# The preparation of a cross-attention and feed-forward kernel, rebuilt: paired 64-row matmuls for K, V and VW, w1 by halves, some parts of the second batch put off, other DMA queues

## The chip, the cores and the metric

The kernel runs on 1 core of a Trainium2 chip. The metric is device time in microseconds (us); lower is better. Before the change the median of 3 runs is 190.82 us (190.44 to 191.01).

## The reference

```python
x = x + xattn(layernorm(x), ctx)      # x (2, 1024, 256), ctx (2, 77, 192)
#   q = x @ Wq (256, 512); k, v = ctx @ Wk, ctx @ Wv (192, 512); 8 heads of 64
#   softmax(q k^T / 8) v, then @ Wo (512, 256) + bo
x = x + ffn(layernorm(x))
#   h = layernorm(x) * gamma + beta
#   y = silu(h @ dequant(fc1_q) + fc1_bias)         # 256 -> 1024
#   x + 0.5 * (y @ dequant(fc2_q) + fc2_bias)       # 1024 -> 256
#   dequant(q, s) = (q - 128) * s, one row of scales for each 128 rows
```

The second layernorm of x stands in front of the ffn, which has one of its own. All is fp32.

## The kernel before

Every engine has its own instruction list written out by hand, and semaphores tie the lists together. A matmul on large operands is made of three with fp32r operands: every operand is split into a rounded part (`_hi`) and what is left (`_lo`), and hi*hi, hi*lo and lo*hi are accumulated. ScalarE (ACT) mostly makes the `_hi` part out of PSUM, and VectorE (DVE) or GpSimd (POOL) subtracts it to give `_lo`.

The 2048 rows of x are eight pieces `a` = 0 to 7 of 256 rows (two tiles j = 0, 1 of 128); pieces 0 to 3 are batch 0, pieces 4 to 7 batch 1. For each piece, TensorE (PE) does XT (transpose x), S (`scores`, 24 matmuls), PT (transpose the probabilities), AO (`attention_out`, 30), HT (transpose the normalised rows hn), F1 (`fc1`, 48) and F2 (`fc2`, 48). The loop runs these in a software pipeline: `fc2` of piece a-1 stands ahead of `scores` of piece a+1.

**Preparation.** Since the context has only 77 rows, the weights are folded once: ctx is transposed (ctxT), K = ctx Wk and V = ctx Wv are made (`project`), Wq is transposed and centred (`transpose_wq`, `sum_wq`, `center_wq`), and then M = Wq K^T (`make_m(b, c)`, batch b, half c of the 256 inputs) and VW = V Wo (`make_vw(b, n)`) for each batch. `scores` then needs only x and M, and `attention_out` only the probabilities and VW. The row bo of the bias is put into VW by two DMAs. The ffn weights w1 and w2 are dequantized (L315 on POOL, L621 on DVE) and split (L439, L489 on ACT; L320 on POOL, L627 on DVE).

Matmuls of the preparation are plain fp32: the trace has two records for each. `make_m` already uses 64 of the 128 rows of the array for each matmul (one head each), in pairs whose two members write different PSUM banks.

PSUM has six named places (S0, S1 of two banks, H0, H1, T0, T1). A table `order` lists who fills each place in turn; `emptied(name)` on PE waits until the previous user was freed by DVE. `fc2(0, 0)` uses T0, which `AO1.0` used before it, and this is freed by `add_attention(1, 0)` (L590) on DVE. In its loop `fc2` waits for `y_lo_done`, the four parts of y_lo that POOL makes (`lower_y`, L310), at its 1st, 7th, 13th and 19th matmul.

Names in the rows: `w_hi`, `w_lo` are w1 or w2, `q_sb` their integers (later the dequantized values), `hT_lo` the lower part of the transposed hn (`split_h`, L607 and L609), `probs` the scores.

## Time and profile before

| | us |
|---|---|
| median of 3 runs | 190.82 |
| profiled execution | 190.24 |
| its span in the trace | 188.5 |
| what lies around the span | 1.74 |

The page counts how long each engine was busy: PE 182.1 us (97%), DVE 123.5 (66%), ACT 122.6 (65%), POOL 115.6 (61%). A busy share over the whole span says nothing about a stage; the views used below are those of stretches, of waits and of single instructions in order of time.

### The profile page before, as it was taken

What the parts mean: (1) busy time and instruction counts of PE and PEld (TensorE: products, weight loads), DVE (VectorE), ACT (ScalarE), POOL (GpSimd) and SP (SyncE); (2) the same over time, 40 slices, a digit from 0 to 9 for tenths busy, and PEclk for the clock granted to TensorE, in tenths of its full rate; (3) what the DMA queues carried; (4) which work ended last, traced back from release to release, by engine and by line L of the source; (5) the groups of instructions that cost most, each with busy time, mean ns of one, the idle gap of its engine ahead of it and who ended that gap; (6) DMA issues with size and microseconds to landing.
All of it is one profiled execution on the core that took longest, in us unless ns stands there. A gap on an engine that the chain in (4) does not pass through costs nothing.

```text
span 188.5 us, 3884 instructions
## 1 busy us (share of the span) xinstructions
PE 182.1 (97%) x1502; PEld 178.2 (95%) x1502; DVE 123.5 (66%) x261; ACT 122.6 (65%) x230; POOL 115.6 (61%) x159
## 2 busy tenths in 40 slices
PE   7999899799899999999999999999999999999994
PEld 7999699699899999999999999999999999998994
DVE  0287988999879374946496459746693768165341
ACT  3287970699728980898288935895389718952580
POOL 5032998479984976298709971697359753767020
PEclk9999999999999999999999999999999999999999
DMA  6996990000000100010001000100000000100101
GB/s 166 331 403 171 354 349 14 2 0 3 2 0 0 59 0 0 3 56 0 3 0 56 3 0 0 47 16 0 3 27 29 0 3 0 56 3 0 56 3 56
DMA packets 9480, 10.72 MB, mean 57 GB/s; under 512 B 2268, under 2 KB 8183, under 8 KB 9335
## 3 DMA queue, kind: packets, MB, share of 16 engines
q1 hardware_dynamic: 8837, 9.70, 15.4%
q10 hardware_dynamic: 626, 0.79, 1.4%
q8 instruction: 12, 0.20, 0.5%
q14 instruction: 5, 0.04, 0.1%
HBM read 8.38 MB, written 2.10 MB: 56 GB/s over the span
## 4 chain that ended last, share of the span: by engine, by line
PE 70%; DVE 10%; POOL 8%; DMA 7%; SPq 2%; issue 1%; ACT 0%
PE H L831 21%; PE T L843 21%; PE S L798 11%; PE T L819 11%; DMA s_sb<-in_L_ffn_fc_scales 7%; PE S L805 3%; PE S L751 3%; POOL w_lo L320 3%; POOL q_sb L315 3%; DVE w_lo L627 2%; DVE hT_lo L609 2%; POOL probs L278 1%; DVE q_sb L621 1%; POOL rstd L289 1%; DVE probs L567 1%
## 5 line engine op out<-in xcount | busy, mean ns | idle before, releaser
L310 POOL TENSOR_TENSOR y_lo<-y,y_hi 128x512 fp32r<-128x512 f32 x28 | 37.6, 1364 | 2.9 <-ACT y_hi L430 2.8
L278 POOL TENSOR_TENSOR probs<-probs,rsum 128x616 f32<-128x616 f32 x16 | 19.1, 1217 | 32.1 <-DVE rsum L579 32.0
L831 PE MATMUL H<-hT_hi,w_hi 128*128 128x256 f32 x128 | 37.3, 291 | 1.3 <-issue 0.8
L843 PE MATMUL T<-w_hi,y_hi 128*128 128x256 f32 x128 | 36.6, 286 | 0.6 <-DVE w_lo L627 0.6
L831 PE MATMUL H<-hT_lo,w_hi 128*128 128x256 f32 x128 | 35.5, 277 | 0.0
L843 PE MATMUL T<-w_lo,y_hi 128*128 128x256 f32 x128 | 35.5, 277 | 0.0
L831 PE MATMUL H<-hT_hi,w_lo 128*128 128x256 f32 x128 | 35.4, 277 | 0.0
L843 PE MATMUL T<-w_hi,y_lo 128*128 128x256 f32 x128 | 35.4, 277 | 0.0
L426 ACT ACTIVATE y<-H,vec 128x256 f32<-128x256 f32 x64 | 26.5, 467 | 8.1 <-PE H L831 8.1
L399 ACT ACTIVATE probs<-probs,rstd 128x616 f32<-128x616 f32 x16 | 12.9, 807 | 27.2 <-DVE probs L567 27.2
L831 PEld LDWEIGHTS H<-hT_hi,w_hi 128*128 128x128 f32 x128 | 24.1, 188 | 2.1 <-issue 1.2
L584 DVE TENSOR_TENSOR pT_lo<-S,pT_hi 128x640 fp32r<-128x640 f32 x16 | 13.1, 822 | 18.9 <-ACT pT_hi L403 18.9
L843 PEld LDWEIGHTS T<-w_hi,y_hi 128*128 128x128 f32 x128 | 24.1, 188 | 0.8 <-DVE w_lo L627 0.8
L843 PEld LDWEIGHTS T<-w_lo,y_hi 128*128 128x128 f32 x128 | 24.1, 188 | 0.0
L831 PEld LDWEIGHTS H<-hT_lo,w_hi 128*128 128x128 f32 x128 | 24.1, 188 | 0.0
L843 PEld LDWEIGHTS T<-w_hi,y_lo 128*128 128x128 f32 x128 | 24.0, 188 | 0.0
L831 PEld LDWEIGHTS H<-hT_hi,w_lo 128*128 128x128 f32 x128 | 24.0, 188 | 0.0
L819 PE MATMUL T<-vw_hi,pT_hi 128*128 128x256 f32 x80 | 22.4, 280 | 0.0
L819 PE MATMUL T<-vw_hi,pT_lo 128*128 128x256 f32 x80 | 22.1, 277 | 0.0
L819 PE MATMUL T<-vw_lo,pT_hi 128*128 128x256 f32 x80 | 22.1, 277 | 0.0
L560 DVE TENSOR_REDUCE smax<-S 128x8 f32<-128x616 f32 x16 | 12.8, 798 | 12.6 <-PE S L798 12.0
L430 ACT ACTIVATE y_hi<-y 128x512 fp32r<-128x512 f32 x32 | 20.2, 632 | 1.0
(127 smaller groups left out, 462.0 us busy)
## 6 DMA issues: line engine op xcount, KB each, us to landing
q_sb<-in_L_ffn_fc_q SPq DMA_DIRECT2D x2, 1024.0 KB, 8.1
out_x<-x_sb SPq DMA_DIRECT2D x16, 128.0 KB, 1.8
x_sb<-in_x SPq DMA_DIRECT2D x7, 256.0 KB, 8.3
s_sb<-in_L_ffn_fc_scales SPq DMA_DIRECT2D x2, 512.0 KB, 11.8
s_sb<-in_L_ffn_fc_scales SPq DMA_DIRECT2D x1, 1024.0 KB, 7.9
wq_sb<-in_L_xattn_Wq SPq DMA_DIRECT2D x1, 512.0 KB, 5.5
wo_sb<-in_L_xattn_Wo SPq DMA_DIRECT2D x1, 512.0 KB, 8.2
wk_sb<-in_L_xattn_Wk ACTq DMA_DIRECT2D x1, 384.0 KB, 4.2
```

Of the source, the lines that this page charges most:

```text
L278: nc.gpsimd.tensor_tensor(p, p, rsum[:, j, :].unsqueeze(2).to_broadcast([P, HEADS, J]), ALU.mult).then_inc(norm_done, 1)
L310: nc.gpsimd.tensor_tensor(y_lo[:, two, :], y[:, two, :], f32(y_hi[:, two, :]), ALU.subtract).then_inc(y_lo_done, 1)
L315: nc.gpsimd.tensor_tensor(w1_sb[:, c, cols], w1_sb[:, c, cols], s1_sb[:, c, cols], ALU.mult).then_inc(w1_done, 1)
L399: nc.scalar.activation(probs[:, j, 0:HJ], probs[:, j, 0:HJ], ACT.Exp, scale=rstd1[:, t:t + 1]).then_inc(exp_done, 1)
L426: ins = nc.scalar.activation(y[:, m, :], r[:, q * W:(q + 1) * W], ACT.Silu, bias=b1_sb[:, m:m + 1])
L430: nc.scalar.activation(y_hi[:, two, :], y[:, two, :], ACT.Copy).then_inc(y_hi_done, 1)
L560: nc.vector.tensor_reduce(smax[:, j, :].rearrange("p (n h) -> p n h", n=2), s, AX_X, ALU.max).then_inc(max_done, 1)
L584: nc.vector.tensor_tensor(flat(pT_lo[:, j, :, :]), ps[bank][:, 0:JC * P], flat(f32(pT_hi[:, j, :, :])), ALU.subtract).then_inc(freed[bank], 1)
L798: ins = mm(o, xt[:, c, j * P:(j + 1) * P], m[:, b, c, h, 0:HALF], start=n == 0, stop=n == len(steps) - 1)
L819: ins = mm(r[:, 0:D], p[:, j, m, :], v[:, b * JC + m, :], start=n == 0, stop=n == len(steps) - 1)
L831: ins = mm(r[:, q * W:(q + 1) * W], wt[:, c, m * P:(m + 1) * P], ht[:, c, :], start=i == 0, stop=i == len(steps) - 1)
L843: ins = mm(o, yt[:, m, j * P:(j + 1) * P], wt[:, m, :], start=m == 0 and i == 0, stop=m == M - 1 and i == 2)
```

## The change

The work on x is not changed. In the preparation:

- `project` makes K (and V) out of 12 matmuls of 64 rows instead of 8 of 96, in pairs on rows 0 to 63 and 64 to 127 that write two PSUM places. For that ctx is loaded with its first 64 columns once more at its end (a second DMA), ctxT has three parts, and wk and wv are loaded in two halves of 64 partitions each.
- `make_vw(b)` is 10 half-row matmuls in five pairs and one full one (`make_middle_vw`), instead of 8 full ones. Heads are stored in another order for this (even heads, then odd ones), in M, probs and VW.
- Order on PE: transposes of Wq, K, XT0, M, V, scores(0), and only then VW of batch 0. Before: K, transposes of Wq, XT0, V, M, half of VW, scores(0), the rest of VW.
- Of batch 1, `make_m(1, 1)` goes to PE's list behind `attention_out(2, 1)`, and its two parts on ACT and DVE with it (`m_hi_part`, `m_lo_part`); the middle of VW goes behind `attention_out(1, 1)`.
- w1 is handled by halves of its 1024 columns; `fc1(0, 0)` waits for the first half only, and `fc2(0, 0)` for the first half of w2. On POOL, one part of w1 is dequantized ahead of the first `normalize` instead of three, and three of the four `lower_w1` come behind the small operations for hn.
- `rsqrt2` is cut in two; its part for the residual goes behind `normalize(1, 1)`.
- DMA: wk and wv on ACT's queue, x(0) on SP's, q1 ahead of x(1); bo and b2 wait for ctx. The two bias rows of batch 0 wait for another part of VW than before (`VW0.1`), which is lowered behind the scores; q2, s2 and the x loads stand behind them on SP.

In every piece: `split_h` signals when its first half is done, and `fc1(f, 0)` starts with its matmuls on that half. At the end, `add_b2(6)` on POOL waits until `split_h(7)` is done.

ACT's list (not in the diff below) follows: `place_v` makes both halves of V on ACT with four copies, DVE copies K's first part instead; `split_w1` comes behind `prob_hi(0, 0)`, `vw_hi_part(1, 0)` and `(1, 1)` behind `hidden(0, 0)`.

The core of the diff, with 12 leading spaces taken off:

```diff
+    sp.dma_start(ctx_sb[:, :, 0:DC], ctx_v).then_inc(ctx_in_sem, 16)
+    sp.dma_start(ctx_sb[:, :, DC:DC + CC], ctx_v[:, :, 0:CC]).then_inc(ctx_in_sem, 16)
     sp.dma_start(wq_sb[:, :, :], wq.rearrange("(n p) f -> p n f", p=P)).then_inc(wq_in, 16)
-    sp.dma_start(wv_sb[:, :, :], wv.rearrange("(n p) f -> p n f", p=CC)).then_inc(wv_in, 16)
+    sp.dma_start(x_sb[:, pair(0), :], x_v[:, pair(0), :]).then_inc(x_in[0], 16)
     sp.dma_start(wo_sb[:, :, :], wo.rearrange("(n p) f -> p n f", p=P)).then_inc(wo_in, 16)
+    sp.dma_start(q1_sb[:, :, :], q1.rearrange("(n p) f -> p n f", p=P)).then_inc(q1_in, 16)
     sp.dma_start(x_sb[:, pair(1), :], x_v[:, pair(1), :]).then_inc(x_in[1], 16)
-    sp.dma_start(q1_sb[:, :, :], q1.rearrange("(n p) f -> p n f", p=P)).then_inc(q1_in, 16)
     for c in range(C):
-        sp.dma_start(s1_sb[:, c, :], s1[c:c + 1, :].to_broadcast([P, F])).then_inc(s1_in, 16)
+        sp.dma_start(s1_sb[:, c, :], s1[c:c + 1, :].to_broadcast([P, F])).then_inc(s1_in[c], 16)
...
-        c, cols = n // 2, slice(n % 2 * F // 2, (n % 2 + 1) * F // 2)
+        c, cols = n % C, slice(n // C * F // 2, (n // C + 1) * F // 2)
...
     nc.gpsimd.tensor_scalar(b2_half[:, :], b2_half[:, :], 0.5, None, ALU.mult).then_inc(b2_done, 1)
-    pool.wait_ge(s1_in, 16 * C)
-    for n in range(2 * C - 1):
-        dequantize_w1(n)
+    pool.wait_ge(s1_in[0], 16)
+    dequantize_w1(0)
     normalize(0, 0)
     normalize(0, 1)
-    dequantize_w1(2 * C - 1)
-    for n in range(2 * C):
-        lower_w1(n)
+    pool.wait_ge(s1_in[1], 16)
+    dequantize_w1(1)
+    dequantize_w1(2)
+    dequantize_w1(3)
+    lower_w1(0)
     rsqrt1(1)
-    rsqrt2(0)
+    rsqrt2_hn(0)
+    lower_w1(1)
+    lower_w1(2)
+    lower_w1(3)
+    normalize(1, 0)
+    normalize(1, 1)
+    rsqrt2_residual(0)
     pool.wait_ge(b2_done, 1)
     for a in range(1, NA):
-        normalize(a, 0)
-        normalize(a, 1)
-        if a < LAST:
-            rsqrt1(a + 1)
+        if a > 1:
+            normalize(a, 0)
+            normalize(a, 1)
         for p in range(HP):
+            if p == (2 if a == 1 else 0) and a < LAST:
+                rsqrt1(a + 1)
             lower_y(a - 1, p)
-        rsqrt2(a)
+        rsqrt2_hn(a)
+        rsqrt2_residual(a)
+        if a == LAST:
+            wait_freed(pool, f"HT{LAST}")
         add_b2(a - 1)
...
-    act.dma_start(wk_sb[:, :, :], wk.rearrange("(n p) f -> p n f", p=CC)).then_inc(wk_in, 16)
-    act.dma_start(x_sb[:, pair(0), :], x_v[:, pair(0), :]).then_inc(x_in[0], 16)
+    for g in range(2):
+        act.dma_start(wk_sb[g * DH:(g + 1) * DH, :, :], wk.rearrange("(n p) f -> p n f", p=CC)[:, :, g * 2 * P:(g + 1) * 2 * P]).then_inc(wk_in, 16)
+    for g in range(2):
+        act.dma_start(wv_sb[g * DH:(g + 1) * DH, :, :], wv.rearrange("(n p) f -> p n f", p=CC)[:, :, g * 2 * P:(g + 1) * 2 * P]).then_inc(wv_in, 16)
+    act.wait_ge(ctx_in_sem, 32)
...
-        ins.then_inc(freed[place[f"HT{a}"][0]], 1)
+            ins.then_inc(h_half_split if c == 0 else freed[place[f"HT{a}"][0]], 1)
...
+    nc.vector.tensor_copy(flat(ctxT[:, 0:2, :]), r[:, 0:2 * BJ]).then_inc(freed["S0"], 1)
     sum_wq(0)
     sum_wq(1)
-    stats1(0)
-    dve.wait_ge(vT_zeroed, 1)
+    place_k0()
+    stats1(0, [0])
     x_lo(0)
-    place_v(0)
-    place_v(1)
     for n in range(4):
         m_lo_part(0, n)
+    stats1(0, [1])
+    shift_scores(0, 0)
+    shift_scores(0, 1)
     dve.wait_ge(bo_hi_done, 1)
     nc.vector.tensor_tensor(bo_lo[:, :], bo_sb[:, :], f32(bo_hi[:, :]), ALU.subtract).then_inc(bo_split, 1)
+    invert_sums(0, 0)
+    vw_lo_part(0, 1)
+    invert_sums(0, 1)
     vw_lo_part(0, 2)
+    x_lo(1)
     vw_lo_part(0, 0)
-    shift_scores(0, 0)
-    shift_scores(0, 1)
-    invert_sums(0, 0)
-    invert_sums(0, 1)
-    vw_lo_part(0, 1)
-    x_lo(1)
+    prob_lo(0, 0)
     m_lo_part(1, 0)
     m_lo_part(1, 1)
-    prob_lo(0, 0)
-    m_lo_part(1, 2)
-    m_lo_part(1, 3)
     prob_lo(0, 1)
-    vw_lo_part(1, 0)
     stats1(1)
     add_attention(0, 0)
     add_attention(0, 1)
...
-    vw_lo_part(1, 1)
-    vw_lo_part(1, 2)
-    stats1(2)
     dve.wait_ge(q2_in, 16)
     dve.wait_ge(s2_in, 16)
     dequantize_w2(0)
+    vw_lo_part(1, 0)
+    vw_lo_part(1, 1)
     dequantize_w2(1)
     prob_lo(1, 0)
     prob_lo(1, 1)
+    stats1(2)
     lower_w2(0)
     lower_w2(1)
     add_attention(1, 0)
     add_attention(1, 1)
+    vw_lo_part(1, 2)
     x_lo(2)
     make_hn(1)
...
+        if a == 2:
+            m_lo_part(1, 2)
+            m_lo_part(1, 3)
         if a < LAST:
             x_lo(a + 1)
...
+    def project(what, weight):
+        names = [f"{what}{g}" for g in range(2)]
+        rs = [emptied(name) for name in names]
+        ins = [None, None]
         for q in range(2):
-            k = 2 * n + q
-            for i in range(2):
-                ins = mm(r[:, q * BJ:(q + 1) * BJ], weight[:, i, k * P:(k + 1) * P], ctxT[:, i, :], start=i == 0, stop=i == 1)
-        fill(f"{what}{n}", ins)
+            for i in range(3):
+                for g in range(2):
+                    rows = slice(g * DH, (g + 1) * DH)
+                    ins[g] = mm(rs[g][:, q * BJ:(q + 1) * BJ], weight[rows, (i + g) % 3, q * P:(q + 1) * P], ctxT[rows, i, :], start=i == 0, stop=i == 2)
+        for g in range(2):
+            fill(names[g], ins[g])
...
+    def make_vw(b):
+        names = [f"VW{b}.{e}" for e in range(2)]
+        rs = [emptied(name) for name in names]
+        steps = [[(m, k, e) for m in range(*vw_chunks[e]) for k, o in sorted(heads_in(m), key=lambda h: key_at(*h))] for e in range(2)]
+        for both in zip(*steps, strict=True):
+            for m, k, e in both:
+                ks = [n for o, n, _ in steps[e] if o == m]
+                rows = slice(e * DH, (e + 1) * DH)
+                q = m - vw_chunks[e][0]
+                ins = mm(rs[e][:, q * D:(q + 1) * D], v_window(k, e, b, m)[rows, :], wo_sb[rows, k, :], start=k == ks[0], stop=k == ks[-1])
+                if (m, k) == steps[e][-1][:2]:
+                    fill(names[e], ins)
+    def make_middle_vw(b):
+        name, at = vw_home(b, 2)
+        k = K - 1
+        mm(emptied(name)[:, at:at + D], v_window(k, 0, b, 2), wo_sb[:, k, :], start=True, stop=True)
...
-            wait_freed(pe, f"HT{f}")
+            pe.wait_ge(h_half_split, f + 1)
         r = emptied(name)
-        steps = [(wt, ht, c) for c in range(C) for wt, ht in ((w1_hi, hT_hi), (w1_hi, hT_lo), (w1_lo, hT_hi))]
-        for q in range(2):
-            m = 2 * p + q
-            for i, (wt, ht, c) in enumerate(steps):
-                ins = mm(r[:, q * W:(q + 1) * W], wt[:, c, m * P:(m + 1) * P], ht[:, c, :], start=i == 0, stop=i == len(steps) - 1)
+        for c in range(C):
+            if p == 0 and c == 1:
+                wait_freed(pe, f"HT{f}")
...
+            if f == 0 and j == 0 and m % (M // 2) == 0:
+                pe.wait_ge(w2_split, m // (M // 2) + 1)
...
     pe.wait_ge(warm_ready, 1)
-    warm(8)
+    warm(6)
     pe.wait_ge(ident_ready, 1)
...
     warm(1)
-    pe.wait_ge(wk_in, 16)
-    wait_freed(pe, "ctxT0")
-    wait_freed(pe, "ctxT1")
-    project("K", 0, wk_sb)
-    project("K", 1, wk_sb)
     pe.wait_ge(wq_in, 16)
     transpose_wq(0)
     transpose_wq(1)
+    pe.wait_ge(wk_in, 32)
+    wait_freed(pe, "ctxT0")
+    wait_freed(pe, "ctxT1")
+    project("K", wk_sb)
     x_transposes(0)
-    pe.wait_ge(wv_in, 16)
-    project("V", 0, wv_sb)
-    project("V", 1, wv_sb)
-    for name in ("K0", "K1", "WQ0", "WQ1"):
-        wait_freed(pe, name)
     for c in range(C):
         make_m(0, c)
+    pe.wait_ge(wv_in, 32)
+    project("V", wv_sb)
+    scores(0, 0)
+    scores(0, 1)
     pe.wait_ge(wo_in, 16)
     wait_freed(pe, "V0")
     wait_freed(pe, "V1")
-    pe.wait_ge(v_even_done, 2)
-    make_vw(0, 2)
-    make_vw(0, 0)
-    scores(0, 0)
-    scores(0, 1)
-    make_vw(0, 1)
+    make_vw(0)
+    make_middle_vw(0)
     x_transposes(1)
     make_m(1, 0)
     pe.wait_ge(probs_ready, 1)
     prob_transposes(0, 0)
-    make_m(1, 1)
     prob_transposes(0, 1)
-    make_vw(1, 0)
     attention_out(0, 0)
     attention_out(0, 1)
     scores(1, 0)
     scores(1, 1)
     h_transposes(0)
-    make_vw(1, 1)
-    make_vw(1, 2)
-    pe.wait_ge(w1_split, 2 * C)
+    make_vw(1)
+    pe.wait_ge(w1_split, C)
     fc1(0, 0)
     fc1(0, 1)
+    pe.wait_ge(w1_split, 2 * C)
+    fc1(0, 2)
     prob_transposes(1, 0)
     prob_transposes(1, 1)
-    fc1(0, 2)
     fc1(0, 3)
     attention_out(1, 0)
     attention_out(1, 1)
+    make_middle_vw(1)
     x_transposes(2)
-    pe.wait_ge(w2_split, 2)
     fc2(0, 0)
     for a in range(2, LAST):
         scores(a, 0)
...
         fc1(a - 1, 3)
         attention_out(a, 0)
         attention_out(a, 1)
+        if a == 2:
+            make_m(1, 1)
```

PE's list from the warm-up matmuls to the first scores, before (T, H and S are the PSUM places):

```order
L736 MATMUL T<-ctxT,wk_sb 128x154 x4
L736 MATMUL H<-ctxT,wk_sb 128x154 x4
L744 MATMUL H<-ident,wq_sb 128x128 x4
L744 MATMUL T<-ident,wq_sb 128x128 x4
L751 MATMUL S<-ident,x_sb 128x128 x4
L736 MATMUL T<-ctxT,wv_sb 128x154 x4
L736 MATMUL H<-ctxT,wv_sb 128x154 x4
L770 MATMUL H<-kT,wqT 128x77
...
L782 MATMUL H<-wo_sb,vT 128x256 x3
L798 MATMUL S<-m_hi,xT_hi 128x308
```

and the same place now:

```order
L799 MATMUL H<-ident,wq_sb 128x128 x4
L799 MATMUL T<-ident,wq_sb 128x128 x4
L790 MATMUL T<-ctxT,wk_sb 128x154
L790 MATMUL H<-ctxT,wk_sb 128x154
...
L806 MATMUL S<-ident,x_sb 128x128 x4
L829 MATMUL H<-kT,wqT 128x77
...
L790 MATMUL T<-ctxT,wv_sb 128x154
L790 MATMUL H<-ctxT,wv_sb 128x154
...
L866 MATMUL S<-m_hi,xT_hi 128x308
```

The transposes of Wq moved ahead of K, and V behind M; VW left the stretch.

POOL's list from the dequantization of w1 to the first lower_y, before (L315 dequantizes, L320 lowers w1, L278 normalizes):

```order
L315 TENSOR_TENSOR q_sb<-q_sb,s_sb 128x512 x3
L278 TENSOR_TENSOR probs<-probs,rsum 128x616 x2
L315 TENSOR_TENSOR q_sb<-q_sb,s_sb 128x512
L320 TENSOR_TENSOR w_lo<-q_sb,w_hi 128x512 x4
...
L291 TENSOR_SCALAR vars<-mv 128x2
...
L278 TENSOR_TENSOR probs<-probs,rsum 128x616 x2
...
L310 TENSOR_TENSOR y_lo<-y,y_hi 128x512 x4
```

and now (L344, L349, L304, L320 and L339 are these lines):

```order
L344 TENSOR_TENSOR q_sb<-q_sb,s_sb 128x512
L304 TENSOR_TENSOR probs<-probs,rsum 128x616 x2
L344 TENSOR_TENSOR q_sb<-q_sb,s_sb 128x512 x3
L349 TENSOR_TENSOR w_lo<-q_sb,w_hi 128x512
...
L349 TENSOR_TENSOR w_lo<-q_sb,w_hi 128x512 x3
L304 TENSOR_TENSOR probs<-probs,rsum 128x616 x2
L320 TENSOR_SCALAR vars<-mv 128x2
...
L339 TENSOR_TENSOR y_lo<-y,y_hi 128x512 x2
```

Two dequantizations went behind the first two normalizations, three lower_w1 behind the operations for hn, and the residual's five small operations (from `vars<-mv 128x2` on) behind normalize(1, 1).

PE's list behind attention_out(2, 1), now; before, the fourth row was not there:

```order
L887 MATMUL T<-vw_hi,pT_hi 128x256
L887 MATMUL T<-vw_lo,pT_hi 128x256
L887 MATMUL T<-vw_hi,pT_lo 128x256
L829 MATMUL S<-kT,wqT 128x77 x8
L806 MATMUL S<-ident,x_sb 128x128 x4
```

make_m(1, 1), 8 matmuls, came in between attention_out(2, 1) and the transposes of x for piece 3.

## Rows read from the trace of the kernel before

**Rows 1.** The page's first line.

```profile
span 188.5 us, 3884 instructions
```

**Rows 2.** Busy time by stretch: start:end, length, then each engine's busy us.

```profile
17.18:48.33 31.15, 29.51 (x232) 27.05 (x230) 29.10 (x54) 22.63 (x42) 26.20 (x28) 1.00 0.32 112
48.84:174.05 125.21, 125.16 (x1056) 124.70 (x1056) 81.73 (x180) 83.79 (x154) 82.99 (x118) 1.00 0.04 14
```

**Rows 3.** Timeline (start, length in us) of DVE and PE, at that stretch's ends.

```profile
17.18 0.80 DVE L560 TENSOR_REDUCE smax<-S 128x8 f32<-128x616 f32 x1 [0.39 <-PE S L798]
...
48.33 0.41 DVE L590 TENSOR_TENSOR x_sb<-T,x_sb 128x256 f32<-128x256 f32 x1
...
48.84 0.36 PE L843 MATMUL T<-w_hi,y_hi 128*128 128x256 f32 x1 [0.56 <-DVE w_lo L627]
```

**Rows 4.** Timeline of PE's weight loads (one for each record) and ACT, preparation.

```profile
7.86 0.49 PEld L744 LDWEIGHTS H<-ident,wq_sb 128*128 128x128 f32 x4
9.19 1.09 PEld L736 LDWEIGHTS T<-ctxT,wv_sb 96*128 96x128 f32 x8
10.14 0.84 ACT L368 ACTIVATE wqT<-T,neg_sum 128x256 f32<-128x256 f32 x2
11.49 0.18 PEld L770 LDWEIGHTS H<-kT,wqT 64*128 64x128 f32 x1 [0.16 <-issue]
11.50 0.18 PEld L770 LDWEIGHTS T<-kT,wqT 64*128 64x128 f32 x1
...
12.38 0.98 PEld L770 LDWEIGHTS S<-kT,wqT 64*128 64x128 f32 x16
13.76 1.27 PEld L782 LDWEIGHTS H<-wo_sb,vT 128*128 128x128 f32 x6
15.10 0.19 PEld L798 LDWEIGHTS S<-m_hi,xT_hi 128*128 128x128 f32 x1
```

**Rows 5.** SP's issue of wq in the timeline, and its landing in the DMA view.

```profile
1.20 0.41 SPq L223 DMA_DIRECT2D wq_sb<-in_L_xattn_Wq  x1
...
wq_sb<-in_L_xattn_Wq SPq DMA_DIRECT2D x1, 512.0 KB, 5.5
```

**Rows 6.** DVE groups by line and shape: busy us, mean ns of one.

```profile
L540 DVE SCALAR_TENSOR_TENSOR m_lo<-H,m_hi 128x308 fp32r<-128x308 f32 x3 | 1.4, 472 | 0.1
L549 DVE TENSOR_TENSOR vw_lo<-T,vw_hi 128x512 fp32r<-128x512 f32 x2 | 1.3, 640 | 0.0
L549 DVE TENSOR_TENSOR vw_lo<-T,vw_hi 128x256 fp32r<-128x256 f32 x2 | 0.8, 410 | 0.0
L647 DVE TENSOR_TENSOR bo_lo<-bo_sb,bo_hi 1x256 fp32r<-1x256 f32 x1 | 0.4, 404 | 0.0
```

**Rows 7.** Timeline of POOL and DVE while w2 is lowered.

```profile
43.80 1.29 POOL L310 TENSOR_TENSOR y_lo<-y,y_hi 128x512 fp32r<-128x512 f32 x1
44.64 1.53 DVE L627 TENSOR_TENSOR w_lo<-q_sb,w_hi 128x1024 fp32r<-128x1024 f32 x1
46.09 2.31 DVE L627 TENSOR_TENSOR w_lo<-q_sb,w_hi 128x1024 fp32r<-128x1024 f32 x1
49.51 1.30 POOL L310 TENSOR_TENSOR y_lo<-y,y_hi 128x512 fp32r<-128x512 f32 x1
```

**Rows 8.** The chain that ended last: pieces of fc1's first half (start, length).

```profile
58.49 2.79 PE H L831 x24
...
138.11 2.87 PE H L831 x24
...
158.07 2.72 PE H L831 x24
```

**Rows 9.** Timeline around the last piece's split_h.

```profile
172.44 1.55 DVE L609 TENSOR_TENSOR hT_lo<-hT,hT_hi 128x256 fp32r<-128x256 f32 x1
...
173.93 0.28 PE L843 MATMUL T<-w_hi,y_lo 128*128 128x256 f32 x1
174.71 0.39 PE L831 MATMUL H<-hT_hi,w_hi 128*128 128x256 f32 x1 [0.50 <-DVE hT_lo L609]
```

212 lines of the change are left out of this document (114 added, 98 removed), and 6 rows, old and new, of the table order.

## The prediction

> **What bounds the kernel now.** I read the page first, for the span [rows 1], then the busy time by stretch. It divides the run into two kinds of time. From 48.84 to 174.05 PE is busy for 125.16 of 125.21 us [rows 2]: nothing but PE's own list sets that time, and a matmul more there costs its full length. Before 48.84 it is otherwise. In the 31.15 us from 17.18 to 48.33 DVE is busy for 29.10, PE for 29.51, POOL for 26.20 [rows 2]; no engine has much to spare. The timeline says which of them ends this stretch: the first matmul of fc2(0, 0), at 48.84, comes 0.1 us behind add_attention(1, 0), which stands last in DVE's list and ends at 48.33 + 0.41 = 48.74 [rows 3]. The bracket names w2's lowering, since that is DVE's row before it, but T0 is freed by the addition. So the preparation is a race of DVE's list, and what is worth something is an earlier start of that list or a shorter one, not less work on PE. The third place where PE waits for another engine is the tail: fc1(7, 0) starts at 174.71, when the matmul before it started at 173.93 [rows 9].
>
> **Start of the scores.** In the list of before, PE makes K while wq is landing (1.20 + 5.5 = 6.7 [rows 5]) and starts the transposes of Wq at 7.86 [rows 4]. Now these come first. With 38 KB more of ctx ahead of wq, and wv beside it on the other queue, I take 7.0 instead of 6.7. From the first transpose to the end of the last centring it took 10.14 + 0.84 - 7.86 = 3.1 us [rows 4], which gives 10.1; the copy of K's second part stands behind it on ACT (0.4, an estimate from the 472 ns of m_lo [rows 6]), but the first matmuls of M need only the first parts. So M starts at 10.3 instead of 11.49. It takes what it took, 12.38 + 0.98 - 11.49 = 1.9, up to 12.2.
>
> V is next. A record of V costs 1.09 / 8 = 136 ns [rows 4]. V was 16 records (2.2 us), and is now 24 in 12 pairs. If the two of a pair run at the same time, this is 12 x 136 ns = 1.65 us; if one after the other, 3.3. The row that speaks for the first is M's: the two members of a pair start 10 ns apart, at 11.49 and 11.50 [rows 4]. I take 1.65; M's low and high parts are ready by then. The scores start at 13.9 instead of 15.10, 1.2 us earlier. If wq comes at 6.7, it is 1.5; if the loads come 1 us late, nothing is left but 0.2.
>
> **From there to fc2(0, 0).** DVE's list gains, between the first smax and add_attention(1, 0), the lowering of VW0 that stood ahead of the scores (640 + 410 ns) and bo_lo (404); it loses two m_lo (2 x 472) and a vw_lo of 256 columns (410) [rows 6]: 1.45 in, 1.35 out, so +0.1. With its waits (31.15 - 29.10 = 2.05 us [rows 2]) as they are, T0 comes free 1.1 us earlier.
>
> POOL is next in line. Its last lower_y of piece 0 ends at 49.51 + 1.30 = 50.81 [rows 7], and fc2(0, 0) needs it at its 19th matmul, 18 x 0.114 = 2.05 us after its start (0.114 is 2.72 / 24 [rows 8]): 48.84 + 2.05 = 50.89. POOL was on time by 0.08 us. Now the residual's five small operations, some 2 us that filled a gap in POOL's time before, stand between normalize(1, 1) and lower_y, and their cover is gone. Against that, normalize(1, 0) starts with DVE's sums, 1.1 earlier, and the waits of before shrink. These waits are seen in rows 7: the first lowering of w2 was given out at 44.64, while POOL's lower_y ran to 43.80 + 1.29 = 45.09, and it ended at 46.17, that is 1.08 us later; the second took 2.31 us, 1.23 more than 1.08. DVE and POOL operations with two operands in SBUF run one after the other here, a whole instruction at a time. Which of them meet depends on the phase, and each meeting is worth up to 1.2 us. I take **-0.7 us** for this stretch, between DVE's -1.1 and POOL's, which is about -0.3; the ends are -1.5 and +1.0 (one more meeting on DVE, and POOL late).
>
> What costs nothing: less work on PE in the preparation (VW 20 half-row records and 2 full ones for 16 of 212 ns, that is 1.27 / 6 [rows 4]) and the halves of w1, since DVE's list sets the end there; if DVE's cover were gone, PE would have 1.5 us to give. The bias rows of batch 0 go out behind the later VW0.1, some 2 us ahead of attention_out(0, 0); if they land late, that start slips by as much. q2 and s2 behind them go out about 5 us later than before and are needed some 14 us after that. The order of heads changes no size.
>
> **make_m(1, 1) behind attention_out(2, 1).** 16 records of the same kind took 0.98 us [rows 4]. There PE has no gap [rows 2], so this is **+1.0 us**. Its two m_hi and two m_lo take 4 x 0.45 on ACT and DVE, which are busy two thirds of that stretch (83.79 and 81.73 of 125.21 [rows 2]); x_lo(3) has fc2(1, 0), 2.7 us, to hide it.
>
> **fc1 on the first half.** In pieces 1 to 5 the first 24 matmuls of fc1 took 2.79 (at 58.49) to 2.87 (at 138.11), five pieces with a sum of 14.33, and 2.72 where hT_lo was done long before (158.07) [rows 8]. 14.33 - 5 x 2.72 = 0.73. In the middle pieces hT_lo ends just when PE arrives. With the first half signalled about 0.65 us earlier most of it goes: **-0.6 us**, between 0 (the wait instruction itself costs it) and -0.75.
>
> **The tail.** hT_lo ran from 172.44 to 173.99 [rows 9], since POOL's add_b2(6) was on its way; add_b2 now waits. PE's previous matmul started at 173.93, so fc1(7, 0) can start at 174.04 instead of 174.71: **-0.7 us**, no more, since PE becomes the bound, and everything behind it moves along. The late add_b2(6) is needed by the two finish_tile(6), which DVE does while it waits for fc1; cover of 2 us.
>
> **Sum.** -0.7 + 1.0 - 0.6 - 0.7 = -1.0 us. The profiled execution took 190.24 (span 188.5 [rows 1] and 1.74 around it) and would take 189.2. It lies 0.58 under the median, and the medians are compared: 190.82 - 1.0 = **189.8 us**.
>
> **A rule that speaks against the loads.** No row has a load into 64 partitions; the loads of wk and wv in this trace go to 96. The Trainium skill ("SBUF — State Buffer", the section on the DMA port swizzle) says that partitions 0 to 63 reach only half of the ports, and gives 196 GB/s at 1 MiB against 328 for 128. By it the 768 KB of wk and wv, in halves, would take 3.9 us of transfer and hold wq up with them; no run here shows it yet.
>
> **The rivals.**
> - *More meetings of DVE and POOL.* split_h(0) now falls into the three lower_w1 on POOL, back to back; a meeting like that of 172.44 costs it 1.2 us, and the sums and normalize(1, 0) with it. Then the first stretch gives +0.5 instead of -0.7: 191.0. For it: rows 7 and 9. Against: DVE's waits of 2.05 us may take it in. Chance 0.16.
> - *Late weights.* If wk, wv or wq land 1.2 us or more later than taken (the two queues share the transfers), the scores start as before, and the stretch gives +0.1 to +0.3: 190.7. Against: wk has nearly the same bytes ahead of it as before. Chance 0.08.
> - *Pairs that don't overlap*, slower than before: K and V take 3.3 us each, M starts 1.5 later than taken and the scores at 17.0, 1.9 later than before; VW0 takes 4.2 instead of 2.1 and holds the first attention_out up by 1 or so. +2.5 + 1.0 - 1.3 = +2.2: 193.0. It decides from a pair that costs over 1.6 records on. Against: the 10 ns of rows 4. Chance 0.08.
> - *Fewer meetings.* POOL's lower_y of piece 0 run ahead of the lowering of w2: -1.5 + 1.0 - 0.7 - 0.7 = -1.9: 188.9. Chance 0.16.
>
> **How the numbers follow.** The forecast has 0.52 and its own range is 189.3 to 190.5. The bound of what a measurement can tell is 0.3%, 0.57 us: faster is below 190.25, slower above 191.4. Faster: 0.8 of the forecast's 0.52 and the 0.16 of fewer meetings, 0.58. Slower: 0.08 and a quarter of the first rival, 0.12. Same: the rest, 0.30. The range of 188.6 to 191.3 leaves out the pairs that don't overlap and the ends of the meetings.
>
> **What the profile after would show.** Scores(0, 0) start near 13.9, and the members of K's and V's pairs start about 10 ns apart (else the third rival). fc2(0, 0) starts near 48.0, with add_attention(1, 0) just ahead of it, and has a gap, if any, before its 13th or 19th matmul (POOL). make_m(1, 1) is about 1.0 us behind attention_out(2, 1) with PE at no wait around it. The pieces of fc1 take 2.72 to 2.75 in the chain. fc1(7, 0) follows its predecessor without a wait, and hT_lo there takes about 0.4. I am wrong above all if fc2(0, 0) starts later than 48.8, or if it starts before 47.

## The result, and the profile after

The changed kernel takes 194.36 us (median of 4 runs, 193.97 to 194.58), the kernel before 190.91 beside it. The ratio is 1.016, with a 95% interval of 1.009 to 1.023. The forecast was 189.8. The change makes the kernel slower by about 3.5 us, and the range of 188.6 to 191.3 does not hold it. Where some executions of a kernel take over 1.5% longer than its fastest, the ratios below leave them out, while the medians count all.

The page's first line of the changed kernel, against 188.5 in [rows 1]:

```profile
span 192.5 us, 3940 instructions
```

The start, in the timeline of PE (start, length in us, what it idled for). Each line stands for as many records as its x says, and the length runs from the first start to the last end:

```profile
4.57 1.00 PE L928 MATMUL S<-ident,ctx_sb 77*128 77x77 f32 x6 [0.60 <-DMA ctx_sb<-in_ctx]
5.36 0.72 PE L779 MATMUL H<-warm_sb 128*128 128x128 f32 x2
7.89 1.11 PE L799 MATMUL H<-ident,wq_sb 128*128 128x128 f32 x4 [1.81 <-DMA wq_sb<-in_L_xattn_Wq]
8.80 1.06 PE L799 MATMUL T<-ident,wq_sb 128*128 128x128 f32 x4
...
10.72 0.46 PE L790 MATMUL T<-ctxT,wk_sb 64*128 64x154 f32 x1
10.73 0.46 PE L790 MATMUL H<-ctxT,wk_sb 64*128 64x154 f32 x1
10.98 0.46 PE L790 MATMUL T<-ctxT,wk_sb 64*128 64x154 f32 x1
...
12.29 0.29 PE L790 MATMUL T<-ctxT,wk_sb 64*128 64x154 f32 x1
12.30 0.29 PE L790 MATMUL H<-ctxT,wk_sb 64*128 64x154 f32 x1
12.42 0.29 PE L790 MATMUL T<-ctxT,wk_sb 64*128 64x154 f32 x1
...
16.94 0.41 PE L866 MATMUL S<-m_hi,xT_hi 128*128 128x308 f32 x1
```

The same view of the kernel before, and from the chain of the changed kernel the landing of Wq (start, length of the transfer):

```profile
7.99 0.60 PE L744 MATMUL H<-ident,wq_sb 128*128 128x128 f32 x4
8.42 0.60 PE L744 MATMUL T<-ident,wq_sb 128*128 128x128 f32 x4
...
15.13 0.44 PE L798 MATMUL S<-m_hi,xT_hi 128*128 128x308 f32 x1
```

```profile
1.55 6.29 DMA wq_sb<-in_L_xattn_Wq
```

Read the starts. The two members of a pair start 10 ns apart, as forecast. But the pairs follow each other every 0.26 us up to about 12.0, and only then every 0.13. The transposes of Wq also take twice what they took before: the second four start 0.91 behind the first, where they started 0.43 behind in the kernel before. TensorE still works at half pace from 7.9 to 12.0, behind a gap of 0.60 and one of 1.81. And Wq comes at 7.85, not at 7.0. The scores start at 16.94, not at 13.9; before, they started at 15.13.

The way from the scores to fc2(0, 0), in the timelines of DVE, POOL and PE:

```profile
34.74 1.48 DVE L650 SCALAR_TENSOR_TENSOR hn<-x_sb,mv,rstd 128x256 f32<-128x256 f32 x1 [0.45 <-POOL rstd L315]
51.65 0.41 DVE L640 TENSOR_TENSOR x_sb<-T,x_sb 128x256 f32<-128x256 f32 x1
```

```profile
34.68 3.90 POOL L349 TENSOR_TENSOR w_lo<-q_sb,w_hi 128x512 fp32r<-128x512 f32 x3
40.87 3.38 POOL L304 TENSOR_TENSOR probs<-probs,rsum 128x616 f32<-128x616 f32 x2 [2.29 <-DVE rsum L629]
44.33 1.25 POOL L320 TENSOR_SCALAR vars<-mv 128x2 f32<-128x2 f32 x1
...
50.73 1.08 POOL L297 TENSOR_SCALAR veps<-mv 128x2 f32<-128x2 f32 x1
...
52.58 2.53 POOL L339 TENSOR_TENSOR y_lo<-y,y_hi 128x512 fp32r<-128x512 f32 x2
```

```profile
52.12 0.38 PE L916 MATMUL T<-w_hi,y_hi 128*128 128x256 f32 x1 [1.25 <-DVE x_sb L640]
54.02 0.36 PE L916 MATMUL T<-w_hi,y_hi 128*128 128x256 f32 x1 [0.22 <-POOL y_lo L339]
55.16 0.39 PE L916 MATMUL T<-w_hi,y_hi 128*128 128x256 f32 x1 [0.20 <-POOL y_lo L339]
55.96 0.30 PE L866 MATMUL S<-m_hi,xT_hi 128*128 128x308 f32 x1
```

The scores of pair 2 in the kernel before:

```profile
51.65 0.30 PE L798 MATMUL S<-m_hi,xT_hi 128*128 128x308 f32 x1
```

DVE's addition, which frees T0, now ends at 52.06 instead of 48.74 [rows 3]. fc2(0, 0) starts behind it at 52.12, and then waits for POOL too: it takes 3.84 us up to the scores of pair 2 (at 55.96), where it took 51.65 - 48.84 = 2.81 before. DVE's second hn took 1.48 beside POOL's lower_w1 (the timeline of before has two in 1.09), and the two normalizations took 3.38 (2.39 before) beside DVE's dequantization of w2. From the scores to DVE's addition it is now 34.71 us (16.94 to 51.65), where it was 33.20 (15.13 to 48.33).

From there on TensorE has no gap, and the chain shows the terms of the loop and the tail:

```profile
62.74 2.73 PE H L902 x24
...
72.71 1.05 PE S L829 x16
...
83.76 2.83 PE H L902 x24
...
103.62 2.72 PE H L902 x24
...
176.35 2.74 PE T L916 x24
179.09 5.44 PE H L902 x48
```

make_m(1, 1) costs 1.05; the five pieces of fc1, three of them shown, sum to 13.72 instead of 14.33 [rows 8]; fc1(7, 0), in the last line, follows fc2 directly. So the whole account of the two profiles is: +1.81 at the start of the scores (16.94 against 15.13), +1.47 from there to fc2(0, 0) (35.18 against 33.71), +1.03 in fc2(0, 0), +1.05 for make_m(1, 1), -0.6 for fc1, -0.7 for the tail. The sum is +4.1; the spans differ by 4.0.

### The profile page after: what moved, and what is told of

It reads as the page before. It is cut to its first block, busy times and chain, and to the rows that moved or that the text cites. A ratio compares the mean times of both kernels' runs of the same rounds, so it can differ in the third digit from the quotient of the medians.

```text
span 192.5 us, 3940 instructions
## 1 busy us (share of the span) xinstructions
PE 182.0 (95%) x1528; PEld 176.5 (92%) x1528; DVE 123.7 (64%) x260; ACT 123.6 (64%) x231; POOL 115.7 (60%) x159
## 4 chain that ended last, share of the span: by engine, by line
PE 75%; POOL 13%; DVE 6%; DMA 3%; issue 1%; SPq 0%; POOLq 0%
PE T L916 21%; PE H L902 20%; PE S L866 13%; PE T L887 11%; PE S L873 3%; DMA wq_sb<-in_L_xattn_Wq 3%; PE S L806 3%; POOL y_lo L339 3%; POOL probs L304 3%; PE T L790 2%; POOL q_sb L344 2%; DVE probs L617 1%; DVE hn L650 1%; PE S L829 1%; POOL rstd L315 1%
## 5 line engine op out<-in xcount | busy, mean ns | idle before, releaser
L304 POOL TENSOR_TENSOR probs<-probs,rsum 128x616 f32<-128x616 f32 x16 | 20.2, 1279 | 35.3 <-DVE rsum L629 35.3
L339 POOL TENSOR_TENSOR y_lo<-y,y_hi 128x512 fp32r<-128x512 f32 x28 | 36.7, 1330 | 2.4 <-ACT y_hi L473 1.9
L902 PE MATMUL H<-hT_hi,w_hi 128*128 128x256 f32 x128 | 36.7, 287 | 0.0
```

The lines of the kernel that those rows point to most:

```text
L304: nc.gpsimd.tensor_tensor(p, p, rsum[:, j, :].unsqueeze(2).to_broadcast([P, HEADS, J]), ALU.mult).then_inc(norm_done, 1)
L339: nc.gpsimd.tensor_tensor(y_lo[:, two, :], y[:, two, :], f32(y_hi[:, two, :]), ALU.subtract).then_inc(y_lo_done, 1)
L902: ins = mm(r[:, q * W:(q + 1) * W], wt[:, c, m * P:(m + 1) * P], ht[:, c, :], start=c == q == i == 0, stop=c == q == 1 and i == 2)
```

## The experiments

All times are medians in us, and the ratios are to the kernel before in the same series. The executions of several kernels spread by 2 to 5 us, so a median there is not to be read finer than about 1 us. A trace shows one execution of them, so its stretches are compared and not its total.

**1. More warming behind ctx.** Behind the transposes of ctx:

```diff
-                warm(1)
+                warm(10)
                 pe.wait_ge(wq_in, 16)
```

> The changed kernel with ten warming matmuls instead of one between the transposes of ctx and those of Wq, so that TensorE has work (some 2 us of it at 0.22 us each) until Wq lands at 7.85; nothing else moves. Theory A (TensorE idled from about 6.1 to 7.9, and then its records came at half pace until 12.0: transposes 0.9 for four instead of 0.44, pairs 0.25 apart instead of 0.13): the Wq transposes take 0.9 together instead of 1.9 and the twelve K pairs 1.6 instead of 2.6, so the first scores start near 15.0 instead of 16.9, and the kernel gains 1 to 2 us: 192.4 to 193.4, by how much of it DVE and POOL hand on. Rival B (the loss is made later, in the lists of DVE and POOL between the first scores and fc2(0,0)): scores start earlier, the time stays within 0.5 of 194.4. Rival C (pairs of 64-row matmuls are slow by themselves): K's pairs stay 0.25 apart and the scores start no earlier than 16.

Measured: 194.29, ratio 1.016 (1.013 to 1.019), scores at 17.00. The run can't weigh theory A against B, since the warming matmuls themselves ran at half pace (20 records in 4.56 us) and pushed the transposes of Wq to 9.66. K's pairs then came 0.13 apart. So rival C (pairs slow by themselves) falls, but more work behind the gap at 4.0, of 0.54 here, did not raise the pace in time.

**2. K ahead of Wq again.**

```diff
-                pe.wait_ge(wq_in, 16)
-                transpose_wq(0)
-                transpose_wq(1)
                 pe.wait_ge(wk_in, 32)
...
                 project("K", wk_sb)
+                pe.wait_ge(wq_in, 16)
+                transpose_wq(0)
+                transpose_wq(1)
```

The copies of K (`place_k0` on DVE, `place_k1` on ACT) move ahead of the sums and the centring of Wq likewise.

> The changed kernel with K's pairs ahead of the transposes of Wq again, as the kernel before has it, on TensorE and in the lists of DVE and ScalarE that read the results. wk lands near 5.6, so K can run while Wq is on its way. Theory A (the order is at fault: it makes TensorE wait 1.8 us for a late Wq and then run at half pace until 12.0): no idle stretch over 0.5 us, K's pairs 0.13 apart (1.6 us), Wq's transposes from 7.9 to 8.8, M from about 11.2, the first scores near 14.8, time 192 to 193. Rival B (lists of DVE and POOL): scores earlier as well, time within 0.5 of 194.4. Rival C (slow pairs): K's pairs 0.25 apart here too, with the first scores at 15.5 or later.

Measured: 195.53 (9 executions, 192.2 to 197.6), ratio 1.006 (1.002 to 1.011). The profiled one was the latest, 197.57: wk in two halves landed only at 7.7, and TensorE waited for it too.

```profile
7.79 0.62 PE L790 MATMUL T<-ctxT,wk_sb 64*128 64x154 f32 x1 [1.59 <-DMA wk_sb<-in_L_xattn_Wk]
```

The order alone is not the cure: against the changed kernel, four executions win 1 to 2 us and five lose 1 to 3.

**3. wv and x(0) on the queues of before.**

```diff
                 sp.dma_start(wq_sb[:, :, :], ...)
-                sp.dma_start(x_sb[:, pair(0), :], ...)
+                for g in range(2):
+                    sp.dma_start(wv_sb[g * DH:(g + 1) * DH, :, :], ...)
...
-                for g in range(2):
-                    act.dma_start(wv_sb[g * DH:(g + 1) * DH, :, :], ...)
+                act.dma_start(x_sb[:, pair(0), :], ...)
```

> The changed kernel with wv's two halves on SyncE's queue behind wq, and x(0) on ScalarE's queue behind wk, as the kernel before has them (wk stays in halves of 64 partitions); the order of work is that of the changed kernel. Theory D (wv's early start on ScalarE's queue is what makes Wq land at 7.85 instead of 6.7): Wq lands by 7.0, TensorE's wait before it shrinks from 1.8 to under 1, and the time falls by 0.8 to 2. Rival E (the second load of ctx and wk in halves hold Wq up, not wv): Wq still lands at 7.6 to 7.9 and the time stays at 194.4 within 0.5.

Measured: 194.66, ratio 1.018 (1.014 to 1.023); Wq landed at 1.55 + 6.4 = 7.95. Theory D falls: it isn't wv's place. Rival E is what is left, the second load of ctx or wk in halves, and no run separates the two. Over the profiles of all kernels here, Wq took 5.5 to 6.5 us from its issue at 1.20 with one load of ctx and wk (six profiles: 6.7 to 7.7), and 6.3 to 7.2 from its issue at 1.55 with two each (eleven profiles: 7.85 to 8.8).

**4. The loop and the tail alone.** The kernel before with the new fc1 and these lines:

```diff
-                    ins.then_inc(freed[place[f"HT{a}"][0]], 1)
+                        ins.then_inc(h_half_split if c == 0 else freed[place[f"HT{a}"][0]], 1)
...
                     rsqrt2(a)
+                    if a == LAST:
+                        wait_freed(pool, f"HT{LAST}")
                     add_b2(a - 1)
```

> The kernel before with only the edits of the loop and the tail: fc1 goes by the first half of h, and POOL's last b2 addition but one waits for the last transposes of h. Nothing of the preparation is changed. By the terms of the prediction (fc1 -0.6, tail -0.7) it gives 190.9 - 1.3 = 189.6; if those two terms were only bought by slack of the new preparation, it stays at 190.9 within 0.4.

Measured: **189.44**, ratio 0.993 (0.989 to 0.996). The two terms are right, and this kernel beats both. The five pieces of fc1 in its chain are 2.72 each, and so the new preparation has no part in that gain. Its way from the scores to the scores of pair 2 (15.87 to 52.44) takes 36.57, as in the kernel before (36.52); in the changed kernel it takes 39.02.

**5. The start of before in the changed kernel.** One load each into 96 partitions, x(0) and wv on the queues of before, eight warming matmuls, K ahead of Wq as in experiment 2, and for K and V:

```diff
-                        for i in range(3):
-                            for g in range(2):
-                                ins[g] = mm(rs[g][:, q * BJ:(q + 1) * BJ], weight[rows, (i + g) % 3, q * P:(q + 1) * P], ctxT[rows, i, :], ...)
+                            for i in range(2):
+                                ins = mm(r[:, q * BJ:(q + 1) * BJ], weight[:, i, k * P:(k + 1) * P], ctxT[:, i, :], ...)
```

M still stands ahead of V.

> The changed kernel with the start of the kernel before: one load each of ctx, wk (96 partitions) and x(0), wv on SyncE's queue, ctx turned in two parts of 96, K and V by 128-column matmuls on 96 rows (16 records each instead of 12 pairs), K ahead of Wq, eight warming matmuls; from M on everything is the changed kernel's. Theory A (1.85 of the loss is a later start, made by TensorE's pace and the late weights, and it is handed on in full): TensorE's pace rises by 6, M starts near 11.0, the first scores near 15.1 instead of 16.9, time 192.3 to 192.9. Rival B (the lists of DVE and POOL behind the scores take the start's gain up in other waits): first scores at 15.1, time above 193.6.

Measured: 196.03, ratio 1.014 (1.006 to 1.023). Four of six executions took 196, with a mean granted clock of 0.982; the other two, at 1.0, took 195.16 and 192.64. In the profiled one (196.08) M started at 11.08 as expected, but the scores only at 17.51:

```profile
8.86 0.60 PE L799 MATMUL S<-ident,x_sb 128*128 128x128 f32 x4
11.08 0.30 PE L822 MATMUL H<-kT,wqT 64*128 64x77 f32 x1 [1.62 <-ACT wqT L407]
...
13.42 2.42 PE L784 MATMUL T<-ctxT,wv_sb 96*128 96x154 f32 x8
15.64 2.26 PE L784 MATMUL H<-ctxT,wv_sb 96*128 96x154 f32 x8
```

Eight records of V take 2.2 here (13.42 to 15.64) and took 1.1 in [rows 4]. The busy time by stretch gives the granted clock in the third number from the end (then DMA share and GB/s); from 13 to 18 it reads 0.50, the level of 1.2 GHz:

```profile
13.00:18.00 5.00, 5.00 (x23) 4.86 (x23) 1.90 (x6) 1.66 (x5) 1.84 (x3) 0.50 0.86 260
```

In the kernel before, V filled the time in which ScalarE centres Wq. With M ahead of V, TensorE idles there for 1.62 us, and then loses its pace. Neither theory A nor B had this. One execution of 192.64 lies in theory A's range; without its trace that is a hint, no more.

**6. The residual's group of POOL ahead of the normalizations.**

```diff
                 lower_w1(3)
+                rsqrt2_residual(0)
                 normalize(1, 0)
                 normalize(1, 1)
-                rsqrt2_residual(0)
```

> The changed kernel with one group of five POOL instructions (variance, power, scale, shift of the residual of pair 0; 2.9 us in the changed kernel, 2.1 in the kernel before) moved from behind the two normalizations of pair 1 to ahead of them, into the 2.3 us for which POOL idles there until 40.87. Theory C (POOL's list between the normalizations and the last y_lo decides when fc2(0,0) ends): y_lo of pair 0 ends near 52.3 instead of 55.1, fc2(0,0) then runs through from 52.1 to 55.1, bounded by DVE's add of the attention, the scores of pair 2 start 1.0 earlier, time 193.4. Rival D (DVE's list decides, and POOL's order is nothing): time within 0.3 of 194.4.

Measured: 193.67, ratio 1.015 (1.010 to 1.020), about 0.7 less than the changed kernel, but two of six executions took 195, so the median alone is not clear of the spread. The trace is: from the scores to the scores of pair 2 it takes 38.37 (18.14 to 56.51) instead of 39.02. This gain of 0.65 is less than 1.0, since DVE's dequantization now met lower_y (2.28 instead of 1.21), and the last two y_lo still waited for the variances of x(2). In this profile the pace had risen behind a gap of 0.58 all the same, and was lost again: Wq came at 8.2, behind an idle time of 2.85, and the granted clock read 0.50 from 9 to 13.

```profile
4.55 0.59 PE L928 MATMUL S<-ident,ctx_sb 77*128 77x77 f32 x6 [0.58 <-DMA ctx_sb<-in_ctx]
```

These six records took 1.00 in the changed kernel.

**7. No gap ahead, and warming until Wq comes.**

```diff
-                warm(6)
+                warm(8)
...
-                warm(1)
+                warm(9)
```

> The changed kernel with eight warming matmuls instead of six ahead of the transposes of ctx, so that TensorE has no gap of 0.6 at 4.0 (the kernel before has eight and no gap), and nine instead of one behind them. Of the run with ten of them behind and six ahead it is known that the warming matmuls themselves went at half pace (0.228 us a record) until about 10 and pushed Wq's transposes to 9.7. Theory E (the pace rises only after TensorE has worked without a gap; the gap at 4.0 lost the rise that the kernel before has at 5.5): the second group goes at 0.11 us a record and is over by 7.4, Wq's transposes start at 7.9 at full pace (0.44 for four), K's pairs are 0.13 apart and done by 10.4, first scores near 14.9, time 192.4 to 193. Rival F (the pace rises late for another reason, such as fewer columns per record or 64-row matmuls): the second group goes at half pace to about 9.5 and the time is 194.4 or more.

Measured: **192.57** (12 runs, 192.19 to 193.21), ratio 1.008 (1.006 to 1.010), 1.8 less than the changed kernel. The timeline of PE:

```profile
1.04 3.79 PE L779 MATMUL H<-warm_sb 128*128 128x128 f32 x16 [1.04 <-DVE warm_sb L684]
4.62 0.98 PE L928 MATMUL S<-ident,ctx_sb 77*128 77x77 f32 x6
5.39 2.40 PE L779 MATMUL H<-warm_sb 128*128 128x128 f32 x18
8.28 0.66 PE L799 MATMUL H<-ident,wq_sb 128*128 128x128 f32 x4 [0.49 <-DMA wq_sb<-in_L_xattn_Wq]
```

The second group of warming matmuls takes 0.13 us a record instead of 0.228, and the transposes of Wq 0.66 instead of 1.11 for four. The scores start at 15.36 although Wq landed 0.4 later than in the changed kernel, and the scores of pair 2 at 54.35 instead of 55.96: an earlier start is handed on in full. Theory E holds as far as the cost of the pace goes; that the pace rises only without a gap does not hold (experiments 6 and 14). Note what this means for the forecast. From the first transpose of Wq to the scores it takes 7.08 at full pace (8.28 to 15.36), and 7.08 to 7.09 in experiments 9, 10, 11 and 15, where the changed kernel took 9.05. The kernel before took 7.14, but its transposes stood behind K and began at 7.99, when Wq had been there since 6.7. The new order ties the scores to the landing itself, and with Wq at 8.2 the new start is not earlier than the old one.

**8. Experiments 5 and 6 together**, with no edit of its own.

> Both edits together: the start of the kernel before (as in the first of these four runs) and the residual's group of POOL ahead of the normalizations of pair 1 (as in the second). Theories A and C together: -1.85 and -1.0, time near 191.5, and what is left over the kernel before (190.9) is make_m(1,1) in the loop (+1.05), meetings of DVE and POOL (+1 to +2), less the gains of fc1 and the tail (-1.2). If only one of them counts, the time is that of the better of the two runs.

Measured: 195.39, ratio 1.022 (1.018 to 1.026). It has experiment 5's idle time and its clock of 0.5, and tells nothing more.

**9. POOL's list and the statistics.** Experiment 7, with the group moved as in 6, and in DVE's list:

```diff
                 invert_sums(1, 1)
+                stats1(2)
...
                 prob_lo(1, 1)
-                stats1(2)
```

> The run with warming matmuls eight and nine (192.57), with the residual's group of POOL ahead of the normalizations of pair 1, and with DVE's statistics of x(2) right behind the reciprocals of pair 1, where the kernel before has them, instead of behind prob_lo(1,1). Theory C2 (what is left of the loss before fc2(0,0) is POOL's list: 2.9 of residual work behind the normalizations, a power that waits for late statistics, and normalizations met by DVE's dequantization of w2): POOL's last y_lo ends by 50.5 instead of 53.5, fc2(0,0) then follows DVE's add of the attention at 50.1 to 50.5 without a break, scores of pair 2 start near 53.5 instead of 54.5, time 191.4 to 191.8. Rival G (the meetings only move to the next instructions of the two engines, as a lengthened dequantization of 2.28 in the run with the residual alone suggests): DVE's add comes later by what POOL gains, the time stays within 0.4 of 192.57.

Measured: 191.91 (12 executions), ratio 1.004 (1.001 to 1.007): 0.7 less than experiment 7, and 1.1 less in the trace from the scores to the scores of pair 2 (37.92, from 38.99). In the timelines of POOL and PE the normalizations are back at 2.39 and fc2(0, 0) has no wait inside:

```profile
39.48 2.39 POOL L304 TENSOR_TENSOR probs<-probs,rsum 128x616 f32<-128x616 f32 x2 [0.33 <-DVE rsum L629]
```

```profile
46.07 0.38 PE L887 MATMUL T<-vw_hi,pT_hi 128*128 128x256 f32 x1 [1.34 <-DVE pT_lo L634]
50.50 0.36 PE L916 MATMUL T<-w_hi,y_hi 128*128 128x256 f32 x1
```

Theory C2 holds in its mechanism, though the last y_lo ends at 51.54 and not by 50.5: the scores of pair 2 start at 53.33. What ends the idle time of TensorE last is now pT_lo(1, 0), behind the two dequantizations in DVE's list, at 46.07; DVE's addition is done at 49.5, with time to spare.

**10. make_m(1, 1) back in the preparation** (experiment 7 as the base), with its high and low parts likewise, and in TensorE's list:

```diff
                 prob_transposes(0, 1)
+                make_m(1, 1)
...
                     attention_out(a, 1)
-                    if a == 2:
-                        make_m(1, 1)
```

> The run with warming matmuls eight and nine (192.57), with make_m(1,1) and its high and low parts back in the preparation, behind the transposes of the probabilities (0,1), instead of behind attention_out(2,1). Theory H (in the loop TensorE has no idle time, so the 1.05 are paid in full; in the preparation it waits for other engines anyway): -1.05 in the loop, +0.4 to +0.9 for the two m_lo parts in DVE's list, time 192.0 to 192.4. Rival I (DVE's list takes all of it, and more where it shifts a meeting): 192.6 or later.

Measured: 193.27 (6 executions, 192.6 to 194.3), ratio 1.012 (1.008 to 1.016), 0.7 more than its base. Rival I holds. From scores to scores of pair 1 it is 15.41 instead of 14.26 us, and the two hn took 2.61. To the scores of pair 2 it is 40.31 instead of 38.99: make_m(1, 1) costs the preparation 1.3, against the 1.05 in the loop. In the profiled execution Wq also came later (scores at 15.92), which may be the rest of the 0.7. So it was no loss that make_m(1, 1) was put off, and hardly a gain.

**11. All repairs.** Experiments 9 and 10 together.

> All repairs of the changed kernel together: warming matmuls eight and nine, residual's group and statistics of x(2) moved as in the first of these four runs, make_m(1,1) in the preparation as in the second. If the terms add up, 192.57 - 1.0 - 0.4 = 191.2, level with the kernel before or 0.3 behind it; the preparation in pairs itself then brings nothing, since with its edits of the loop and the tail (-1.3) the kernel before runs at 189.4. If the pairs of the preparation do bring what was forecast, it is below 190.

Measured: 191.99, ratio 1.004 (1.002 to 1.007), no better than experiment 9. Here too make_m(1, 1) costs the preparation what it saves in the loop: to the scores of pair 2 it is 39.06, against 37.92 in experiment 9. The repaired new preparation stays 2.5 us behind the old one with the same loop and tail (189.44).

**12. Three more edits on experiment 4.** fc2(0, 0) waits for w2 by halves, rsqrt1(2) stands behind two y_lo, and in DVE's list:

```diff
                 lower_w2(0)
+                add_attention(1, 0)
                 lower_w2(1)
-                add_attention(1, 0)
```

> The kernel before with the edits of the loop and the tail (189.44 in its run), and three more small ones at its bound before fc2(0,0): fc2(0,0) waits for w2 by halves, DVE adds the attention of tile (1,0) between the two halves of w2's low part, POOL takes the variances of pair 2 behind two y_lo parts instead of ahead of all four. In the kernel before TensorE waits from 48.28 to 48.84 and runs without a gap from there: theory: fc2(0,0) starts 0.5 earlier, time 188.9. Rival: y_lo's last part or a meeting with DVE takes it back, 189.4 or later.

Measured: 191.95, ratio 1.002 (0.999 to 1.006), worse than experiment 4. Five executions took 190.2 to 190.8 and seven 191.9 to 192.5; the profiled one is of the seven (192.25). The rival holds, and in this trace by its meeting: POOL's y_lo now runs beside the dequantization of w2.

```profile
41.46 4.34 DVE L623 SCALAR_TENSOR_TENSOR q_sb<-q_sb,s_sb 128x1024 f32<-128x1024 int32 x2
```

It took 2.35 before. TensorE then idles for 1.81 until 46.59, and from 48 to 50 the granted clock reads 0.50, so that attention_out of pair 1 takes 5.31 in the chain, where it takes 3.80 in experiment 9. The fall comes to some 1.5 of the 2.75 by which the way from the scores to the scores of pair 2 grew against experiment 4 (39.32, from 36.57). The chain, and the busy time by stretch:

```profile
46.59 5.31 PE T L821 x30
```

```profile
48.00:50.00 2.00, 2.00 (x12) 2.00 (x11) 1.25 (x3) 1.95 (x5) 1.53 (x2) 0.50 0.00 0
```

**13. Eight warming matmuls, nothing else**, in the changed kernel:

```diff
-                warm(6)
+                warm(8)
```

> The changed kernel with eight warming matmuls instead of six ahead of the transposes of ctx, nothing else; behind them stays the one, so that TensorE still waits some 1.8 to 2.5 us for Wq. Theory E1 (the gap at 4.0 alone keeps the pace low): Wq's transposes and K's pairs go at full pace at once (0.44 for four, 0.13 a pair), first scores at 15.1, time near 192.6. Theory E2 (the wait of about 2 us for Wq lets the pace fall again, as in the trace of the run with the residual's group moved, where the granted clock read 0.50 from 9 to 13 behind a wait of 2.85): K's pairs are 0.25 apart and the granted clock reads 0.5 there, time 194 or more.

Measured: 193.94, ratio 1.012 (1.007 to 1.018), executions from 192.5 to 195.8, the profiled one the latest. Theory E2 holds in the trace: the pace has risen by 5.0 and falls again behind the wait for Wq. Four of the other five executions have a mean granted clock of 0.991 and took 193.8 to 194.4; the one at 0.999 took 192.49, which is near the 192.6 of theory E1. PE's timeline, and the busy time by stretch:

```profile
5.00 0.43 PE L779 MATMUL H<-warm_sb 128*128 128x128 f32 x2
8.39 1.12 PE L799 MATMUL H<-ident,wq_sb 128*128 128x128 f32 x4 [2.97 <-DMA wq_sb<-in_L_xattn_Wq]
```

```profile
9.00:12.00 3.00, 3.00 (x20) 2.67 (x20) 1.38 (x2) 1.65 (x4) 0.00 (x0) 0.50 1.09 334
```

The same stretch in the changed kernel, which works at half pace there too, reads 1.00:

```profile
9.00:12.00 3.00, 3.00 (x21) 2.67 (x21) 1.38 (x2) 1.68 (x4) 0.00 (x0) 1.00 1.10 333
```

**14. Six warming matmuls in the kernel before.**

```diff
-                warm(8)
+                warm(6)
```

> The kernel before with six warming matmuls instead of eight ahead of the transposes of ctx, nothing else (the mirror of the run before this one). Theory E (the gap ahead of ctx's transposes is what costs the rise): K's records of 154 columns 0.25 apart instead of 0.14 for some time behind 5.8, the first scores 1 to 2.5 later than 15.1, time 192 to 193.5. Rival F (the changed kernel's low pace came from its own matmuls of 64 rows or its late weights): nothing moves, 190.9 to 191.1.

Measured: 192.60, executions from 190.6 to 193.8, ratio 1.004 (1.000 to 1.008). The profiled execution was one of the quick ones (191.4): behind a gap of 1.07 its pace had risen all the same. So the gap doesn't always cost the rise. Over all executions the edit costs 1.7 in the median; that the later ones lost it by their pace is likely, and no trace of one was taken.

**15. The residual's group right behind rsqrt2_hn(0)**, otherwise experiment 9.

```diff
                 rsqrt2_hn(0)
+                rsqrt2_residual(0)
                 lower_w1(1)
                 lower_w1(2)
                 lower_w1(3)
-                rsqrt2_residual(0)
```

> The run with warming matmuls eight and nine and the moved statistics of x(2) (191.9), with the residual's group of POOL right behind rsqrt2_hn(0), where the kernel before has it, instead of ahead of the normalizations of pair 1: the small POOL instructions then stand beside DVE's second hn, and lower_w1(1) to (3) follow. Theory M (the second hn takes 1.48 instead of 0.5 because lower_w1 of 128x512 runs beside it, and everything behind it on DVE is late by that): hn of about 0.5, transposes of h 0.9 earlier, DVE's add of the attention 0.9 earlier, time 191.0. Rival N (lower_w1 meets the next DVE instructions instead, or fc1(0,2) and the normalizations wait for POOL): 191.6 to 192.

Measured: 193.34, ratio 1.011 (1.006 to 1.016), 1.4 worse than experiment 9. The second hn takes 0.48 as theory M says, but rival N decides, and beyond its range of 191.6 to 192, since fc1(0, 0) then waits for the w1_lo that POOL makes 2.1 us later:

```profile
38.46 0.36 PE L902 MATMUL H<-hT_hi,w_hi 128*128 128x256 f32 x1 [1.47 <-POOL w_lo L349]
```

## Why the prediction was wrong

- **Start of the scores: this step failed, by two terms.** It took 7.0 for Wq's landing and TensorE's full pace, and came to 13.9. The pairs overlap as assumed (10 ns, 0.13 us a pair once the pace is up), and what stands behind the landing was sized well: 6.9 taken, 7.1 measured at full pace (experiments 7, 9, 10, 11 and 15). But Wq landed at 7.85 here, and at 7.85 to 8.8 over the eleven profiles with the changed loads; 0.35 of that is its later issue, behind the second load of ctx. And the pace, which the forecast had no term for, was half from 7.9 to 12.0: 9.05 from the first transpose to the scores instead of 7.1. That is +0.9, +2.0 and +0.2 on the 13.9. Experiment 7 sets the price of the pace in the time at 1.8 us. Even there the scores start at 15.36, still behind the 15.13 of before, since nearly all of the gain of 1.2 stood on the landing. The +0.2 is K's second part: M waits for its copy after all (done at 11.65 in experiment 7, M at 11.80), where the forecast let it start without.
- **Late weights:** this rival had the landing (1.2 or more later than taken, scores as before), which is what the traces at full pace show. It had a chance of 0.08 and nothing of the pace.
- **The rule on ports.** The prediction cited the Trainium skill ("SBUF — State Buffer", on the DMA port swizzle) against loads into 64 partitions, and left it out of the sum. The landings agree in direction: Wq about 1 us later in the mean of the profiles with halves (8.26 against 7.23), and wk's second half landed as late as 7.7 in one, where one load into 96 partitions was there by 4.9 to 5.6. Experiment 3 excludes wv's place; whether it is the ports, the second load of ctx or the more numerous short packets was not separated.
- **From there to fc2(0, 0), -0.7: this step failed too, and in sign.** Apart from the earlier start, the list of DVE was to take 0.1 more; it took 1.5 more, and fc2(0, 0) 1.03 more inside. The waits were taken as they were before, and they changed: the second hn met lower_w1 (+1.0) and the normalizations met the dequantization of w2 (+1.0). The rival of more meetings named this mechanism, with split_h in the place of hn, but gave the stretch +0.5 where it became +2.5. The sentence on POOL, that the residual's five operations have lost their cover, was right. It was priced at some 0.4 (-0.7 instead of -1.1), while POOL's list held fc2(0, 0) up by the 1.03; experiment 6 gives 0.7 back. Experiments 9, 12 and 15 show that such a meeting is moved more easily than removed.
- **make_m(1, 1), +1.0:** measured +1.05 in the loop. What it spares the preparation was counted only as two m_lo in DVE's list; experiments 10 and 11 show 1.3 and 1.1 for it, so that the move is about even.
- **fc1, -0.6, and the tail, -0.7:** measured -0.6 and -0.7; both alone, in experiment 4, -1.4 by the ratio and -1.7 by the medians.
- **Pairs that don't overlap:** this rival came nearest with its time (193.0) and its start of the scores (17.0), and for the wrong reason: that is luck.

What stays open: the last 1.4 us or so between the repaired new preparation (191.9) and the old one with the same loop (189.4), beyond the 1.05 of make_m(1, 1). The traces place it between the scores and the scores of pair 2 (37.92 in experiment 9, 36.57 in experiment 4). Most of it is likely DVE's list between 33 and 46 with its 1.48 hn, and no experiment removed it without a new wait.

## What to carry to other kernels

Before moving a load's consumer to the front of TensorE's list, ask what it did while that load was on its way, and take a range for the landing, not one profile's number: a filler that looks like work on the path (K, then V) may be free and also keep the clock up. The later start was handed on in full here; what a new order of the lists of VectorE and GpSimd gives is only what their next meeting leaves of it. Take the edits apart: here two of them were worth 1.4 us by themselves, and were hidden under a loss of 5.4.

## What the runs showed of the hardware

- TensorE starts at half pace: 20 warming records of 128 columns took 4.56 us in experiment 1, and 18 took 2.40 in experiment 7, most of them behind the rise. In the eleven profiles in which it worked from 1.04 on without a gap, the pace rose between 3.9 (experiment 4) and 6.9 (experiment 12). With a gap of 0.5 to 1.1 near 4.0 it rose at 12.0 in the changed kernel and at 10 or later in experiments 1, 2 and 3, but was up right behind the gap in experiments 6 and 14.
- The column of the granted clock reads 1.00 in that first half-pace time (9 to 12 in the changed kernel), so the starts of equal records have to be read. Once the pace has risen, a fall does show there as 0.50 (1.2 GHz). It fell behind idle times of 1.62, 1.81, 2.85 and 2.97 (experiments 5, 12, 6 and 13), and did not behind one of 1.72 in the profile of experiment 10, so the length of an idle time alone does not tell.
- The Trainium skill ("TensorE: Matmul & The Clock Gate", the part on the HAM clock gate) names two levels, 1.2 and 2.4 GHz, and a cold start, and the traces agree. On the same page of the Trainium skill, the section on oscillation describes waits for DMA that let the clock fall. Here waits of 2.85 and 2.97 us for Wq did that, and so did waits for other engines: 1.62 for ScalarE, with M's short records of 64 rows following it, and 1.81 for VectorE.
- Two-operand instructions of VectorE and GpSimd that ran beside each other took longer: the second hn 1.48 instead of 0.48 (the changed kernel and experiment 15), a pair of dequantizations between 2.35 (experiment 4) and 4.34 (experiment 12), two hn between 0.98 (experiment 12) and 2.61 (experiment 10). Moving one by a microsecond changed others by 1 to 2 us.
